# Gated linear attention and feed-forward on one core: the norms before the feed-forward grouped at the end of VectorE's queue, the first update of k moved to VectorE, the rounding of `w_ff2` moved one slot on

## The reference, cut to what matters

```python
x = x + layernorm(attn(layernorm(x)))        # gated linear attention, 4 heads
x = x + layernorm(ffn(layernorm(x)))         # expert ffn: w2(gelu(w1 x + b1)) + b2

# attention, per head: q, k of 64 features, v of 128, g = log_sigmoid(...) / 16
S = exp(g_t)[:, None] * S + k_t[:, None] * v_t[None, :]
o_t = q_t @ S
# then an RMS norm of o, times silu(x @ Wg), times Wo
```

## Time and profile before

| What | Value |
|---|---|
| median of 3 runs | 1180.05 us (1177.93 to 1180.56) |
| the profiled execution | 1180.13 us, its span 1178.4 us |
| PE busy | 1102.3 us (94%) |
| PEld busy | 915.3 us (78%) |
| DVE busy | 869.9 us (74%) |
| ACT busy | 813.5 us (69%) |
| POOL busy | 631.4 us (54%) |
| granted clock of TensorE, mean | 0.987 |
| chain that ended last, by engine | PE 59%, ACT 18%, DVE 14%, issue 6%, POOL 3% |

### The profile page before, as it was taken

How to read it: one execution, slowest core, us unless ns; L and a number is a source line. 1 busy time by engine, 2 the same in 40 slices (tenths; PEclk the granted TensorE clock), 3 DMA queues, 4 the chain that set the end, 5 groups by cost and what they waited for, 6 DMA issues and landing times.

```text
span 1178.4 us, 31971 instructions
## 1 busy us (share of the span) xinstructions
PE 1102.3 (94%) x12624; PEld 915.3 (78%) x12624; DVE 869.9 (74%) x1973; ACT 813.5 (69%) x1749; POOL 631.4 (54%) x938
## 2 busy tenths in 40 slices
PE   4799999999999999999999999999999999999967
PEld 3686878878787887878878787887878778787856
DVE  4748679686877858678686877868688685877763
ACT  5586767777577686866778676787757767686633
POOL 6457356464555644566445645547455564456631
PEclk9799999999999999999999999999999999999989
DMA  4010010100110001100011001010011100110000
GB/s 150 3 36 20 19 55 7 55 20 19 55 60 19 3 18 56 59 20 19 11 47 59 21 19 55 3 58 20 19 55 45 34 3 18 56 60 2 20 1 18
DMA packets 32148, 38.87 MB, mean 33 GB/s; under 512 B 2752, under 2 KB 29440, under 8 KB 32000
## 3 DMA queue, kind: packets, MB, share of 16 engines
q1 hardware_dynamic: 31472, 36.30, 9.4%
q10 hardware_dynamic: 528, 0.52, 0.1%
HBM read 28.43 MB, written 8.39 MB: 31 GB/s over the span
## 4 chain that ended last, share of the span: by engine, by line
PE 59%; ACT 18%; DVE 14%; issue 6%; POOL 3%; DMA 0%; DVEq 0%; POOLq 0%; ACTq 0%
PE ps_big L265 14%; PE ps_big L266 11%; PE ps_big L267 11%; DVE q_blockdiag L678 4%; ACT square_out L995 3%; PE ps_out L495 3%; PE ps_level L265 3%; PE ps_level L320 2%; PE ps_level L267 2%; PE ps_level L266 2%; PE ps_transpose L509 2%; PE ps_transpose L275 2%; DVE h_lo L683 2%; DVE xT_lo L648 2%; ACT L1087 2%
## 5 line engine op out<-in xcount | busy, mean ns | idle before, releaser
L1230 POOL TENSOR_TENSOR k_decayed<-k_decayed,block_totals 128x256 f32<-128x256 f32 x192 | 149.7, 796 | 163.2 <-PE ps_level L320 121.9
L678 DVE TENSOR_TENSOR q_blockdiag<-q_blockdiag,block_totals 128x512 f32<-128x512 f32 x192 | 171.7, 907 | 2.5 <-PE ps_level L301 2.3
L1236 POOL TENSOR_TENSOR rstd<-mean_var,minus_half 128x1 f32<-128x1 f32 x192 | 109.3, 572 | 86.2 <-DVE mean_var L716 86.2
L265 PE MATMUL ps_big<-w_ff_hi,h_hi 128*128 128x256 f32 x512 | 150.5, 294 | 1.4
L266 PE MATMUL ps_big<-w_ff_lo,h_hi 128*128 128x256 f32 x512 | 144.6, 282 | 0.0
L267 PE MATMUL ps_big<-w_ff_hi,h_lo 128*128 128x256 f32 x512 | 144.6, 282 | 0.0
L265 PE MATMUL ps_big<-xT_hi,w_ff_hi 128*128 128x512 f32 x256 | 109.6, 428 | 18.5 <-DVE xT_lo L648 18.5
L940 ACT ACTIVATE ps_transpose<-ps_big,ff_b_cols 128x512 f32<-128x512 f32 x128 | 84.7, 662 | 52.5 <-DVE h_lo L683 29.7
L1260 POOL TENSOR_TENSOR w_ff_lo<-w_raw,w_ff_hi 128x256 fp32r<-128x256 f32 (+1 forms) x96 | 107.9, 1141 | 5.5 <-ACT w_ff_hi L932 5.5
L265 PE MATMUL ps_big<-w_vg_hi,xT_hi 128*128 128x512 f32 x256 | 109.5, 428 | 0.7
L265 PEld LDWEIGHTS ps_big<-w_ff_hi,h_hi 128*128 128x128 f32 x512 | 97.7, 191 | 7.4 <-DVE h_lo L683 3.8
(11 more groups left out here) (134 smaller groups left out, 3171.9 us busy)
## 6 DMA issues: line engine op xcount, KB each, us to landing
w_raw<-L_ffn_w SPq DMA_DIRECT2D x16, 1024.0 KB, 6.2
out<-y SPq DMA_DIRECT2D x16, 512.0 KB, 3.5
x_in<-L_attn_x SPq DMA_DIRECT2D x15, 512.0 KB, 3.9
ff_b_rows<-L_ffn_b SPq DMA_DIRECT2D x8, 128.0 KB, 2.2
x_in<-L_attn_x ACTq DMA_DIRECT2D x1, 512.0 KB, 4.4
w_raw<-L_attn_Wv SPq DMA_DIRECT2D x1, 512.0 KB, 5.6
w_raw<-L_attn_Wg SPq DMA_DIRECT2D x1, 512.0 KB, 7.5
y<-L_attn_Wo SPq DMA_DIRECT2D x1, 512.0 KB, 8.4
```

Of the source, the lines that this page charges most:

```text
L265: nc.tensor.matmul(out, ah, bh, start=(first and i == 0), stop=False)
L678: nc.vector.tensor_tensor(q, q, t.to_broadcast([P, 2, T // (2 * h), h]), ALU.mult)\
L1230: nc.gpsimd.tensor_tensor(k, k, t.to_broadcast([P, m, h]), ALU.mult)\
L1236: nc.gpsimd.tensor_tensor(rs[:, k, c:c + 1], mv[:, k, c, 1:2], mhalf[:, 0:1], ALU.pow)\
```

## The change

Four things are done:

- On VectorE the tail is put in another order. `ln2(2)` stands ahead of `q_times_k(0)`, `normed_attn(2)` behind `og_lo(3)`, `ln2(3)` ahead of `q_times_gate(1)`. Then come `normed_attn(3)`, the four `ln3_stats` and the four `ln3`, all in the same slot.
- On GpSimd the tail has `residual(2)`, the last block totals, `rsqrt(1, 3)`, `residual(3)` and then the four `rsqrt(2, c)`.
- The two updates of k at level 0 are made by VectorE (`first_k_update`), each between `copy_pairs(0, tl)` and `q_update(0, tl)` at the start of the slot. The semaphore `dv_ku` tells TensorE of them, and `po_ku` counts the other levels alone.
- `weight_hi(1)` goes from the end of the even slot to the start of the odd slot, behind the two `xT_hi` and the copy of the diagonal's row, ahead of `gelu(0)`. It waits for the `f2` of the slot before that one.

```diff
--- before.py
+++ after.py
@@ -161,7 +161,7 @@
             ac_x3hi=KT, ac_gelu=FT, ac_hhi=FT, ac_ws=2,
 
 
-            po_p1=1, po_p2=NCH, po_p3=NCH, po_p4=NCH, po_x2=NCH, po_fin=NCH, po_tot=NL, po_ku=2 * NL,
+            po_p1=1, po_p2=NCH, po_p3=NCH, po_p4=NCH, po_x2=NCH, po_fin=NCH, po_tot=NL, po_ku=2 * (NL - 1), dv_ku=KT,
             po_ro=2 * NCH, po_w1=4, po_w2=8,
         )
         sem = {n: ctx.enter_context(nc.semaphore(n)) for n in PER}
@@ -282,7 +282,10 @@
 
                 def level(i, tl):
                     pe.wait_ge(sem["dv_qu"], at("dv_qu", s, 2 * (i - 1) + tl + 1))
-                    pe.wait_ge(sem["po_ku"], at("po_ku", s, 2 * (i - 1) + tl + 1))
+                    if i == 1:
+                        pe.wait_ge(sem["dv_ku"], at("dv_ku", s, tl + 1))
+                    else:
+                        pe.wait_ge(sem["po_ku"], at("po_ku", s, 2 * (i - 2) + tl + 1))
                     if i - 1 < MASKED:
                         pe.wait_ge(sem["dv_cp"], at("dv_cp", s, 2 * (i - 1) + tl + 1))
                     else:
@@ -291,7 +294,7 @@
 
                 def top_level():
                     pe.wait_ge(sem["dv_qu"], at("dv_qu", s, 2 * NL - 2))
-                    pe.wait_ge(sem["po_ku"], at("po_ku", s, 2 * NL - 2))
+                    pe.wait_ge(sem["po_ku"], at("po_ku", s, 2 * (NL - 2)))
                     pe.wait_ge(sem["ac_cp"], at("ac_cp", s, 8))
                     for tl in range(KT):
                         for c in range(NCH):
@@ -374,7 +377,7 @@
                     last.then_inc(sem["pe_f2"], 1)
 
                 def kh(f):
-                    pe.wait_ge(sem["po_ku"], at("po_ku", s, 2 * NL))
+                    pe.wait_ge(sem["po_ku"], at("po_ku", s, 2 * (NL - 1)))
                     if A:
                         pe.wait_ge(sem["dv_xlo"], at("dv_xlo", n, f + 1))
                     elif C:
@@ -678,6 +681,12 @@
                     nc.vector.tensor_tensor(q, q, t.to_broadcast([P, 2, T // (2 * h), h]), ALU.mult)\
                         .then_inc(sem["dv_qu"], 1)
 
+                def first_k_update(tl):
+                    dve.wait_ge(sem["pe_lv"], at("pe_lv", s, tl + 1))
+                    k = kk[:, tl, :].rearrange("p (n t) -> p n t", t=2)[:, :, 0]
+                    t = ga[:, tl, :].rearrange("p (n t) -> p n t", t=2)[:, :, 1]
+                    nc.vector.tensor_tensor(k, k, t, ALU.mult).then_inc(sem["dv_ku"], 1)
+
                 def h_lo_part(m):
                     dve.wait_ge(sem["ac_hhi"], at("ac_hhi", p, m + 1))
                     nc.vector.tensor_tensor(h_lo[:, m, :], PT[m % 2][:, :], h_hi[:, m, :].bitcast(F32),
@@ -764,9 +773,9 @@
                     dve.wait_ge(sem["po_x2"], at("po_x2", s, c + 1))
                     stats(2, x2[:, c, :], c, "dv_ln3", s)
 
-                def ln3(c, b):
-
-                    dve.wait_ge(sem["po_p3"], at("po_p3", b, c + 1))
+                def ln3(c):
+
+                    dve.wait_ge(sem["po_p3"], at("po_p3", s, c + 1))
                     nc.vector.tensor_scalar(xh[:, c, :], x2[:, c, :], mv[:, 2, c, 0:1], rs[:, 2, c:c + 1],
                                             ALU.subtract, ALU.mult).then_inc(sem["dv_xh3"], 1)
 
@@ -798,13 +807,13 @@
                     nc.vector.scalar_tensor_tensor(qg[:, tl, :], PB[tl][:, :], QSCALE, ga[:, tl, :],
                                                    ALU.mult, ALU.mult).then_inc(sem["dv_q"], 1)
 
-                if C:
-                    ln3(3, p)
                 for i in range(NL):
                     for tl in range(KT):
                         if B:
                             if i < MASKED:
                                 copy_pairs(i, tl)
+                            if i == 0:
+                                first_k_update(tl)
                             q_update(i, tl)
                         if C and i + tl == 0:
                             for kt in range(KT):
@@ -875,30 +884,28 @@
                     og_lo(2)
                     og(3)
                     normed_attn(1)
+                if B:
+                    ln2(2)
                 if A:
                     q_times_k(0)
                 if B:
                     og_lo(3)
+                    normed_attn(2)
                 if A:
                     q_times_gate(0)
-                if B:
-                    ln2(2)
-                if A:
                     q_times_k(1)
+                if B:
+                    ln2(3)
+                if A:
                     q_times_gate(1)
                     if not B and not C:
                         dve.wait_ge(c_ready, 3)
                 if B:
-                    ln2(3)
-                    normed_attn(2)
-                    ln3_stats(0)
-                    ln3_stats(1)
                     normed_attn(3)
-                    ln3_stats(2)
-                    ln3(0, s)
-                    ln3(1, s)
-                    ln3_stats(3)
-                    ln3(2, s)
+                    for c in range(NCH):
+                        ln3_stats(c)
+                    for c in range(NCH):
+                        ln3(c)
 
             program(dve, run)
 
@@ -946,8 +953,10 @@
 
                     W, cols = ((W1, DF), (W2, D))[c]
                     act.wait_ge(sem["w_in"], at("w_in", en, 16 * (c + 1)))
-                    if C:
-                        act.wait_ge(sem[("pe_f1", "pe_f2")[c]], at(("pe_f1", "pe_f2")[c], p, (FT, NCH)[c]))
+                    if c == 0 and C:
+                        act.wait_ge(sem["pe_f1"], at("pe_f1", p, FT))
+                    elif c and p:
+                        act.wait_ge(sem["pe_f2"], at("pe_f2", p - 1, NCH))
                     copy(W[0][:, :, :], raw[:, :].rearrange("p (k n) -> p k n", n=cols), "ac_ws")
 
                 def copy_blocks(i, tl):
@@ -1037,6 +1046,8 @@
                     act.wait_ge(sem["pe_drow"], at("pe_drow", s, 1))
                     copy(o[:, 0, 0:CH], PO[:, 0:CH], "ac_dg")
                 if C:
+                    if j == 1:
+                        weight_hi(1, e)
                     act.wait_ge(sem["b_in"], at("b_in", e, 32))
                 for i in range(1, NL):
                     if B and not C and i <= NCH:
@@ -1130,9 +1141,6 @@
                     v_evac(3, n)
                 if V:
                     g_evac(3, n)
-                if A and j == 0:
-                    weight_hi(1, 0 if not C else e + 1)
-
             program(act, run)
 
         @block.gpsimd
@@ -1220,10 +1228,10 @@
                         nc.gpsimd.tensor_tensor(totals(2 * LV[i]), t[:, :, :, 0], t[:, :, :, 1], ALU.mult)\
                             .then_inc(sem["po_tot"], 1)
 
-                def k_update(i, tl, b):
+                def k_update(i, tl):
 
                     h = LV[i]
-                    pool.wait_ge(sem["pe_lv"], at("pe_lv", b, 2 * i + tl + 1))
+                    pool.wait_ge(sem["pe_lv"], at("pe_lv", s, 2 * i + tl + 1))
                     m = T // (2 * h) - (CH // (2 * h) if i == NL - 1 else 0)
                     k = halves(kk[:, tl, :], h)[:, 0:m, 0, :]
                     t = totals(h)[:, tl, :].rearrange("p (n t a) -> p n t a", t=2, a=1)[:, 0:m, 1, :]
@@ -1264,8 +1272,8 @@
                 next_e = 0 if not C else e + 1
                 for i in range(1, NL):
                     if B:
-                        k_update(i, 0, s)
-                        k_update(i, 1, s)
+                        k_update(i, 0)
+                        k_update(i, 1)
                     if C and j == 1 and i < 5:
                         weight_lo(1, 2 * i - 2, e)
                         weight_lo(1, 2 * i - 1, e)
@@ -1308,20 +1316,14 @@
                 if A:
                     block_totals([5])
                 if B:
+                    residual(2)
+                if A:
+                    block_totals([6])
+                if B:
                     rsqrt(1, 3, "dv_ln2", s, "po_p2")
-                    residual(2)
-                    rsqrt(2, 0, "dv_ln3", s, "po_p3")
                     residual(3)
-                    rsqrt(2, 1, "dv_ln3", s, "po_p3")
-                    rsqrt(2, 2, "dv_ln3", s, "po_p3")
-                if A:
-                    block_totals([6])
-                    pool.wait_ge(sem["po_tot"], at("po_tot", n, NL))
-                    k_update(0, 0, n)
-                if B:
-                    rsqrt(2, 3, "dv_ln3", s, "po_p3")
-                if A:
-                    k_update(0, 1, n)
+                    for c in range(NCH):
+                        rsqrt(2, c, "dv_ln3", s, "po_p3")
 
             program(pool, run)
```

More of the change, by code:

```diff
@@ L881, in run @@
                     og_lo(3)
+                    normed_attn(2)
                 if A:
                     q_times_gate(0)
+                    q_times_k(1)
                 if B:
-                    ln2(2)
+                    ln2(3)
                 if A:
-                    q_times_k(1)
                     q_times_gate(1)
```

4 lines of the change are left out of this document (2 added, 2 removed).

## The result

The changed kernel takes 1158.58 us (median of 4 runs, 1156.52 to 1160.29) against 1180.01 us. The ratio is 0.9821, with a 95% interval of 0.9801 to 0.9841: it is faster, by 21.4 us. The forecast was 1161.3 us with a range of 1157.5 to 1168.0. The profiled execution is the longest of the four, 1160.29 us with a span of 1158.6; that is 19.8 us less than the profiled execution of the kernel before, where the sum said 18.8.

The account below looks back on a forecast made before the run. TensorE is fullest and loses time idling at slot openings, set by the start of `xT_hi`. Savings of 8 x 1.60 = 12.8, 7 x 0.76 = 5.3 and 0.7 give 18.8 off 1180.13: 1161.3 us, range 1157.5 to 1168.

Parts of the forecast that it names:

- the sum: Even slots' ends save 12.8 us, odd slots' 5.3, the last tail 0.7: together 18.8 off 1180.13.
- costs TensorE 0.22 us per tail: VectorE's new tail order makes `gp(2)` start at 584.27, not 584.05; bounds 0 and 0.5.
- The low end of the range: If the tail cost TensorE nothing: gains of 1.82 and 0.98 per opening, 22.6 us in all, so 1157.5.
- Cost: nothing: VectorE's two added updates of k fit into idle time each slot; at the upper end about 0.3 us per slot.
- my two signs of being wrong that belong together: At the slot's opening: the copy of level 1 shows no idle time ahead of it, and level 2 a wait.
- The cover that I worked out: Slack for the second update of k: 0.09 us to spare at level 1's copy, a further 0.17 at level 2.
- The first rival: VectorE pays for the updates of k, 0.3 us in each of 15 slots: 1165.8 us; chance 0.13.
- the last tail: Slot 15, without projections to hide behind: the new order gains 0.7 us, bounds 0 and 1.1.
- the tail held TensorE longer: Waits at `gp(2)` and `wo(3)` cost 0.7 us, not 0.22, per tail: 1168.4 us; chance 0.09.
- GpSimd's power of chunk 2: Slower rival: this power reaches `normed_attn(2)` late and delays the rest of the tail, 1184.9 us at 1.5 late; chance 0.03.
- bound elsewhere in the opening: Norms come first but gain nothing, only the rounding counts, 8 x 0.8 = 6.4 us: 1173.7; chance 0.05.
- The k rival: VectorE pays 0.3 us per slot for the updates of k, 4.5 in all: 1165.8 us; chance 0.13.

Follow-up runs that it names:

- e1: The kernel before with only the rounding of `w_ff2` moved; 1171.50 us, ratio 0.9940.
- e7: The changed kernel with `ln2(2)`, `normed_attn(2)` and `ln2(3)` back behind what TensorE waits for, norms still grouped, GpSimd's chunk 3 power ahead of `residual(2)`; 1154.17 us, ratio 0.9792.
- e6: The changed kernel with a second, equal VectorE operation ahead of each first update of k; 1160.51 us, ratio 0.9840.
- e3: The changed kernel with the two first updates of k given back to GpSimd, behind its four powers; 1158.60 us, ratio 0.9831.
- e4: The kernel before with the updates of k moved to VectorE and the rounding moved, the order of the norms left as before; 1158.31 us, ratio 0.9826.
- e2: The changed kernel with the rounding put back at the end of the even slot's ScalarE queue; 1178.97 us, ratio 0.9994.
- e5: The kernel before with only the two updates of k moved to VectorE; 1175.91 us, ratio 0.9978.
- e9: The changed kernel with the rounding put back and 16 unread TensorE transposes filling the gap before `f1(0)` in odd slots; 1174.96 us, ratio 0.9971.

## Why the prediction was right

**The norms.** The wait for `x_normed` went in fifteen of sixteen places. I put the last `x_normed` 0.7 to 1.2 us ahead of TensorE; it is 1.46. The reason that I gave for the opening, that the start of `xT_hi` sets it, is shown by e1: with the rounding out of the way `xT_hi` follows `x3t`, and 0.81 comes out where the rule gives 0.81.

**The rounding.** It takes 1.93, ends 0.48 before it would matter, and costs nothing. Behind an even slot 1.60 was saved (70.70 to 69.10), behind an odd slot 0.78 (69.71 to 68.93); the sum had 1.60 and 0.76.

**A mis-sized term that was made good by another, by luck.** The term "costs TensorE 0.22 us per tail" is 0.33: the two waits and the slower start behind the second (e7). The gains came out right all the same, since `xT_hi` starts 0.50 behind the last gate's start when it is queued (581.03, 581.53), and I had counted 0.62, the time from the gate's start at 518.89 until the rounding started in the earlier trace rows. The errors, 0.11 and 0.12, have opposite signs; that they cancel was no merit of the working. The low end of the range, 1157.5, rested on a tail that costs nothing. The kernel with such a tail, e7, takes 1154.2: it gains 1.92 and 1.13 per opening, where I had 1.82 and 0.98.

**The updates of k.** Each takes 0.45, and I had 0.41 from the earlier trace rows and 0.34 of queue time for 0.37. "Cost: nothing" holds; e6 shows that even twice the work would cost 0.05 in every second slot. Of my two signs of being wrong that belong together one came, no idle time ahead of the copy of level 1, but level 2 showed no wait. The cover that I worked out (0.09 and 0.17) was too small. The first rival is out by that and by e3. "GPSIMD Engine Reference" of the Trainium skill names, in Key points, contention with instructions of two SBUF inputs. The q update of e3 is one and shows it (1.11 beside an update of k, 0.68 without); the last `x_normed` of e3, with one tensor input, was slowed as well (0.95 for 0.41). None of it lay on the path, and the moved updates met none in the opening shown: the one behind `xT_lo` starts at 583.60, just as GpSimd's own update ends (582.85 + 0.74).

**What I did not say.** The parts are not terms of a sum. By the medians the rounding alone is worth 8.2 us, k 2.9, norms and k together 0.7, and all three 21.4. By the traces, from the first `x3t` with a feed-forward to the last `f1(0)`, it is 6.5, 2.1, 0.15 and 18.3; the lower clock behind the long gap is in the second and third. The rounding covered what the norms won behind even slots, and the norms covered all but 0.81 of what the rounding could win. That norms and k are substitutes (e3, e4) my text did not see: it gave the whole gain to the new order and none to moving k, while either would have been enough, and the new order costs 0.33 per slot for TensorE.

**The size.** By the traces, `f1(0)` of the last slot comes 19.2 us earlier (1146.12 against 1126.95): 8 x 1.60, 7 x 0.78 and 0.8 for the last tail are 19.1. The last 0.6 us of the profiled span are the clock. In the last slot it comes back to its higher level earlier in the changed kernel. Windows from `f1(0)` on, of the changed kernel first and then of the kernel before:

```profile
1126.95:1131.00 4.05, 4.05 (x10) 3.19 (x11) 0.00 (x0) 1.00 (x2) 0.00 (x0) 0.50 0.00 0
1131.00:1136.00 5.00, 5.00 (x23) 4.08 (x22) 2.08 (x3) 3.93 (x7) 0.00 (x0) 0.96 0.00 0
```

```profile
1146.12:1150.00 3.88, 3.88 (x9) 3.11 (x10) 0.00 (x0) 0.84 (x2) 0.00 (x0) 0.50 0.00 0
1150.00:1155.00 5.00, 5.00 (x19) 3.96 (x19) 1.78 (x3) 3.28 (x6) 0.00 (x0) 0.80 0.00 0
```

The average over five microseconds is 0.96 after and 0.80 before. The median gained 1.6 us more than the profiled pair, whose second member is the slowest of its four. The four go with their mean granted clock: 1160.29 at 0.987, 1158.67 and 1158.49 at 0.988, 1156.52 at 0.991. No trace shows where in the other three the clock was higher.

The other rivals: the tail held TensorE longer than I said, by 0.11 and not by 0.5. GpSimd's power of chunk 2 came in time (e7 differs from the changed kernel by no more than the two waits). And TensorE was not bound elsewhere in the opening.

**Slips in my sums.** By their own terms, 590.18 to 590.20 plus 0.22 give 590.40 to 590.42, not 590.43. The k rival's 0.3 per slot is 0.25 (0.85 - 0.43 - 0.17), so its 4.5 is 3.8. The tail is bounded by 0.5 in one place and 0.4 in another; these give 1165.5 and 1164.0, and I wrote 1165. The first moves the forecast by at most 0.2 us, the others do not touch it.

## What to carry to other kernels

Where several engines reach one point at nearly the same time, change them together or reckon with a gain of nothing: price each part by the start of the one event that all of them feed, not by its own idle time. When work is brought forward, look at what stood in front of it: grouping the norms was free for them and cost TensorE 0.33 us per slot, because two of its feeders were pushed behind them, and putting these back gave 4.6 us more over fourteen slots. And two short stalls that merge to a long one can cost more than their sum: 0.97 and 1.49 us left the clock alone here, and 2.49 in one piece did not, in two slots of seven.

## What the runs showed of the hardware that I had not expected

- Idle times of TensorE of 0.97 and 1.49 us, with 1.9 us of work between them, left the granted clock at 2.4 GHz in all slots of the kernel before. One of 2.5 to 2.7 us was followed in some slots, two of seven in each of two traces, by a mean of 0.65 to 0.67 over 4 to 5 us, and cost 1.3 to 1.4 us each time. Which gaps it strikes I can't tell from the traces. Over its ten runs e2 had mean granted clocks of 0.982 to 0.987 and e5 of 0.980 to 0.986, against 0.987 to 0.989 in the eight of e9.
- A product of TensorE behind a wait took 0.11 us more until the next one started (0.34 for 0.23). The same 0.34 stands behind a change of form with no wait shown: the product at 577.36, behind the 32 small ones of a level, is followed at 577.70.
- On VectorE, 0.37 us of added work moved the end of the chain that it feeds by 0.04: the copy came only 0.16 later, so 0.2 of idle time was used up, and the operation behind it ran shorter (1.01 for 1.10), with less of it beside GpSimd's update of k (0.47 for 0.55).
- In the first 37 us of a trace the granted clock differs between executions, 0.77 or 0.89 from 22 to 37 us, and with it the time at which the full slots begin.
